# Local attention: the fourth spreading of key factors one step later, as the first dense product of step 14

## The reference

```python
qkv = shift_token(x) @ wqkv                    # 128 -> 3 x 512: 8 heads of 64
q, k, v = split(qkv)
q = l2norm(q) * qs
k = l2norm(k) * ksc
q, k = rotary_xpos(q, k)
o = local_attention(q, k, v)                   # window of 64, looks one window back, softmax
x = x + o @ wo
h = layernorm(shift_token(x)) ; h = h @ w1 + b1 ; a, g = split(h)
x = x + (a * gelu(g)) @ w2 + b2
```

## Time and profile before

| what | value |
|---|---|
| median of the runs | 4783.61 us (3 runs, 4780.45 to 4787.08) |
| the profiled execution, its own time | 4792.77 us |
| its span | 4791.0 us |
| mean granted clock of TensorE | 0.90 of full speed |
| first pass of the local attention | about 762 to 1272 us of the span |
| second pass | about 1804 to 2312 us |

### The profile page before, as it was taken

How to read it: one execution, slowest core, us unless ns; L and a number is a source line. 1 busy time by engine, 2 the same in 40 slices (tenths; PEclk the granted TensorE clock), 3 DMA queues, 4 the chain that set the end, 5 groups by cost and what they waited for, 6 DMA issues and landing times.

```text
span 4791.0 us, 62689 instructions
## 1 busy us (share of the span) xinstructions
PE 4206.6 (88%) x23278; PEld 2009.3 (42%) x23280; DVE 3025.6 (63%) x6690; ACT 2453.2 (51%) x4189; POOL 1123.7 (23%) x1579
## 2 busy tenths in 40 slices
PE   8888879999898889999886777999888999889999
PEld 5212335555522235555552224555553334333343
DVE  4888467667478867776345994666666653466622
ACT  3587634455348774554345553455444663236642
POOL 1100123333210013333112662111121004420034
PEclk9799987899879998998797998999997999969999
DMA  1100102111010011111000000000001000000000
GB/s 49 27 15 14 45 3 73 28 36 35 6 55 18 15 49 36 32 34 28 5 7 5 0 0 16 8 16 8 16 33 27 22 8 1 29 22 21 15 0 9
DMA packets 48017, 104.07 MB, mean 22 GB/s; under 512 B 15064, under 2 KB 15064, under 8 KB 46432
## 3 DMA queue, kind: packets, MB, share of 16 engines
q1 hardware_dynamic: 46560, 98.49, 7.5%
q10 hardware_dynamic: 1152, 1.57, 0.1%
HBM read 40.24 MB, written 1.05 MB: 9 GB/s over the span
## 4 chain that ended last, share of the span: by engine, by line
PE 62%; DVE 23%; ACT 8%; POOL 3%; issue 2%; DMA 1%; ACTq 1%; SPq 0%; POOLq 0%; DVEq 0%
PE PS L447 29%; PE PS L1123 8%; PE PS L1071 7%; DVE SM L1197 6%; PE PS L1103 3%; PE PS L2638 2%; DVE AR L2442 2%; ACT AR L454 2%; DVE AR L451 2%; PE PS L1741 1%; PE PS L1751 1%; PE PS L474 1%; PE PS L1076 1%; ACT AR L1171 1%; PE PS L1744 1%
## 5 line engine op out<-in xcount | busy, mean ns | idle before, releaser
L1197 DVE TENSOR_REDUCE SM<-PS 128x1 f32<-128x512 f32 (+3 forms) x1792 | 1028.3, 626 | 241.1 <-PE PS L1071 160.3
L447 PE MATMUL PS<-AR,WS 128*128 128x512 f32 (+1 forms) x2112 | 1058.1, 640 | 77.1 <-DVE AR L451 30.8
L1171 ACT ACTIVATE AR<-PS 128x1024 f32<-128x1024 f32 (+3 forms) x896 | 825.5, 933 | 342.5 <-PE PS L1106 171.6
L454 ACT ACTIVATE AR<-PS 128x512 f32<-128x512 f32 (+4 forms) x728 | 440.5, 614 | 523.4 <-PE PS L447 395.2
L1071 PE MATMUL PS<-AR 51*128 51x512 bf16 (+3 forms) x1792 | 527.6, 391 | 142.3 <-DVE SM L1197 98.9
L447 PEld LDWEIGHTS PS<-AR,WS 128*128 128x128 f32 (+1 forms) x2112 | 401.4, 202 | 539.0 <-issue 407.7
L1822 ACT ACTIVATE AR<-PS,SM 128x128 f32<-128x128 f32 x512 | 229.6, 452 | 475.3 <-DVE SM L1885 471.2
L1123 PE MATMUL PS<-AR 128*32 128x512 f32 (+3 forms) x3584 | 451.3, 577 | 1.3 <-ACT AR L1171 0.9
L1071 PEld LDWEIGHTS PS<-AR 51*128 51x128 bf16 x1792 | 130.0, 94 | 661.5 <-DVE SM L1197 476.2
L1103 PE MATMUL PS<-AR 51*128 51x512 bf16 (+3 forms) x1792 | 387.2, 367 | 11.8 <-ACT AR L1171 11.0
L1230 POOL CAST MBT<-SM 128x8 bf16<-128x8 f32 x128 | 28.0, 219 | 1262.7 <-DVE SM L1201 1065.8
(11 more groups left out here) (323 smaller groups left out, 7183.5 us busy)
## 6 DMA issues: line engine op xcount, KB each, us to landing
TP<-RAW SPq DMA_DIRECT2D x512, 64.0 KB, 2.0
AR<-AR SPq DMA_DIRECT2D x720, 32.0 KB
WS<-wall SPq DMA_DIRECT2D x4, 3654.5 KB, 11.2
WS<-wall SPq DMA_DIRECT2D x8, 902.5 KB, 4.5
WS<-wall SPq DMA_DIRECT2D x2, 3334.5 KB, 10.6
WS<-wall SPq DMA_DIRECT2D x1, 2384.0 KB, 9.2
WS<-wall SPq DMA_DIRECT2D x1, 1543.5 KB, 6.1
AR<-AR ACTq DMA_DIRECT2D x48, 32.0 KB
```

Source lines behind the costliest of these rows:

```text
L447: t = e.matmul(o, l, r, start=(n == 0), stop=(n == len(pairs) - 1))
L454: return e.activation(o, i, ACT.Copy, scale=1.0)
L1171: e.activation(pv[:, :, off:512], sv[:, :, off:512], ACT.Exp, scale=scale).then_inc(*F.at_exp.up((s, u, p2)))
L1197: e.tensor_reduce(mh[:, at, k0 // 512:k0 // 512 + 1], bank(ring(n + g), m), AX.X, ALU.max, negate=True).then_inc(*F.at_max.up((s, k, i, rr ...
```

## The change

For groups 1 to 7 `wide` 3 goes from `second` of step 13 to `first` of step 14. Group 0, which is prepared before the first unit, keeps its four in steps 13 and 14.

```diff
@@ -1622,10 +1622,15 @@
                 second = [("norm", g, j) for j, at in enumerate((2, 3, 4, 4, 6, 7, 10, 11)) if n == at] + second
                 if n == 11:
                     first += [("turn", g, 0)]
-                wide = 12 if g else 13
-                if n in (wide, wide + 1):
-                    first += [("wide", g, 2 * (n - wide))]
-                    second += [("wide", g, 2 * (n - wide) + 1)]
+                if n == 12 and g:
+                    first += [("wide", g, 0)]
+                    second += [("wide", g, 1)]
+                if n == 13:
+                    first += [("wide", g, 2 if g else 0)]
+                    second += [] if g else [("wide", g, 1)]
+                if n == 14:
+                    first += [("wide", g, 3 if g else 2)]
+                    second += [] if g else [("wide", g, 3)]
                 second += [("v", g, j) for j, at in enumerate((8, 11, 14, 15) if g else (8, 11, 12, 12)) if n == at]
```

## The result

The changed kernel takes 4754.6 us (median of 5 runs, 4750.2 to 4771.9) against 4783.9 us before (5 runs, 4780.5 to 4787.7): ratio 0.9949, 95% interval 0.9935 to 0.9963. A second set, taken beside the first experiments, gave 4761.8 us (12 runs, 4755.5 to 4775.8) against 4777.2 us (25 runs, 4764.2 to 4790.5): ratio 0.9970, interval 0.9958 to 0.9982. So the kernel is faster, by 29 us in one set and by 15 us in the other.

What follows compares the result with a forecast made beforehand. TensorE, 88% busy, was taken as the bound, waiting 27.3 us for VectorE's key products. Wait -21.1, border +1, clock -7 give -27.1 us; from the 4783.6 us median that makes 4756.5 us, range 4741 to 4773.

Steps and rivals of the forecast that it cites:

- The order and the removed wait: Steps 13 and 14: fourth spreading moves behind step 14's scores; TensorE's 27.3 us of key-product waits go or fall near 1 us.
- The second condition, the copy: Step 14's transposes must await VectorE's copy of step 13, so the shown group gains 1.8 us, not 1.95.
- The border: Product 3 in step 15 delays the next group's first scores, mostly hidden: 1 us for 14 borders, at most 10.
- The clock: Low clock from step 13 on ends 1.8 us sooner per group, 23 us in all; at 0.3 that gains 7 us.
- the 21.1 us: TensorE's gain from the removed wait over 14 groups, limited by the copy; bounds about 12 and 27.3 us.
- The low stretch halved: Rival: low-clock time from step 13 on halves, gaining 22 us instead of 7, total 4741.5 us; chance 0.15.
- That the clock would not move: Rival: the same light steps remain, transposes do not raise the clock, so no clock gain, 4763.5 us; chance 0.18.
- VectorE as the bound: Rival: border costs 10 us and step 15's copy delays step 0's transposes 7 us; 4779.5 us, no change; chance 0.11.
- The slower case: Rival: low clock spreads over whole groups, 5.9 us each; with seven of fourteen hit, 4805 us; chance 0.04.

Runs made afterwards that it cites:

- bank4: Kernel before, instruction order unchanged, with only the fourth spreading of groups 1 to 7 put in PSUM bank 4: 4758.2 us, ratio 0.9953.
- step14_double: Kernel before with product 3 computed twice in VectorE's step 14, once into a scratch tile: 4781.7 us, ratio 1.0008.
- again: The changed kernel, unaltered, measured once more beside the other experiments against the kernel before: 4761.8 us, ratio 0.9970.
- before_fill: Kernel before with five unused matmuls on TensorE ahead of the fourth spreading in groups 1 to 7: 4765.0 us, ratio 0.9962.

## Why the prediction was right, point by point

**The forecast** was 4756.5 us with a range of 4741 to 4773; the two sets gave 4754.6 and 4761.8. In differences, 27.1 us were forecast and 29 and 15 measured. Both times lie inside the range. That the first set met the forecast within 2 us is in part luck: two terms of the sum were wrong in opposite directions, as said below, and the same program gained half as much in the second set.

**The order and the removed wait.** As forecast: 27.3 us of waits for the key products became 9.8 us in all. I had expected "near 1 us"; 8.4 us remain for product 0 (11.1 in the second set), since the scores and values of step 14 ran at the higher clock and TensorE reached the moved spreading sooner than at the 2.21 us that I took from the earlier trace rows. In the shown group scores and values took 1.4 us (934.25 to about 935.65) and the spreading waited for product 0 to end.

**The second condition, the copy.** This step of the working decided, and as a bound it held. Forecast for the shown group: transposes of step 14 right behind the copy, 1.8 us gained. Measured: 0.14 us behind the copy's end, steps 13 and 14 in 8.04 us instead of 9.86, 1.8 us less. bank4 showed the same bound with another cure, 1.52 us of wait for the copy. Over all 14 groups steps 13 and 14 went from 131.2 to 106.2 and 107.4 us, 25.0 and 23.8 us less, where the sum said 21.1. But only a small part of that is idle time saved. In the shown group TensorE idled 1.95 us before and 0.93 + 0.64 = 1.57 us after; the scores and values between took 1.4 us instead of 2.21, at the higher clock. Of its steps 13 and 14 some 8.2 us had the low clock before and 2.6 us after. Over all groups the low clock in these two steps fell from 95 us to 46 and 40.

**The border.** The waits of the first scores are 1.4 us in 9 times, at most 0.2 each where up to 0.7 was forecast; the cost was put at 1. That they are hidden behind ScalarE's copy fits the shown group, where its wait shrank from 0.53 to 0.16 us; over both passes that wait (L1751, then L1756, for L454) went from 18.7 us in 26 times to 17.3 in 30. Counted from the weight loads, step 15 became longer (43.0 us in all groups before, 49.3 and 50.5 after) and step 0 shorter (52.7, then 41.8 and 46.6), but that is mostly where the count puts the border: before, the weight load of step 0's mask ran ahead of its matmul (956.25 and 956.68 in the shown group), and now it waits with it for product 3 (943.59 and 943.62). From mask matmul to mask matmul step 15 took 47.8 us before, 47.4 and 49.4 after, and step 0 45.7, then 41.0 and 45.4.

**The clock.** The term was too small, by the amount of low clock and not by its price. I took the low stretch to end 1.8 us sooner, 23 us of low clock in all, and argued that the clock falls before the wait, so that taking the wait away does not keep it high. In the traces it is the start that moved: before, in 11 of the 14 groups the low stretch began at most 2.3 us behind the start of step 13, or earlier; in the changed kernel that was so in 5 groups and in 2, and in the others it began 4.3 us or more behind it, in step 14. The passes had 168 and 206 us of it against 250, and against 207 in the profile of the kernel with product 3 twice, which has the same order. So the low clock saved is anything from 0 to 82 us, by the pair that one takes; in steps 13 to 0 alone it is 41 to 64 us. The price taken, 0.3 us per us, is near the 0.31 (13.4 us for 43, the kernel before against its double) to 0.44 us that pairs of like programs show; the 0.18 that stood at its lower end came from two groups of unlike work (477 and 499 matmuls).

What the change saves without the clock comes out alike in two estimates. At equal low clock over the passes (step14_double and again, 207 and 206 us, though spread otherwise: 126 and 85 us of it in steps 13 to 0) it is 1003.9 - 994.9 = 9.0 us; and the idle time in the rows of waits fell by 11.0 us, in the second set by 27.3 - 11.1 - 1.5 - (11.9 - 5.1) = 7.9 us. With the 0.34 us per us of before_fill, an estimate for the passes is 11.0 + 82 x 0.34 = 38.9 us (measured 39.0) and 7.9 + 44 x 0.34 = 22.9 us (measured 22.4). So about half or more of the 21.1 us that I booked as the wait's own length is the clock's: it was reckoned with step 14 at 1.2 GHz as it stood in the trace, and before_fill shows that this clock goes with the wait. The sum came out because what one term had too much the other had too little. (Its lower bound, given as about 12 us, is 21.1 - 10 = 11.1; the range goes by 11.)

**The rivals.** The low stretch halved (0.15) is nearly what happened to the clock (139 to 75 and 85 us in steps 13 to 0), but not to the time, since the 21.1 us beside it held the clock already and TensorE at the higher clock ran into waits for VectorE: 8.4 us for product 0 and 6.5 us more for the copy. That the clock would not move (0.18) is not borne out in the moved steps, where the low clock fell in both profiles; over the whole passes the second profile's 206 us are no less than the 207 of step14_double, so there it can't be excluded. The Trainium skill, "TensorE: Matmul & The Clock Gate", Part 4 (PE-mode transpose), has it that transposes do not count towards the full clock; what moved up was scores, a spreading and transposes, and the low clock of these steps fell all the same. No run isolates the transposes, so the rule itself is not tested. VectorE as the bound (0.11), by a border that costs its full 10 us, did not come; VectorE does bind step 14, through the copy. The slower case (0.04), low clock over whole groups, did not come; the one group that had it lost it (69.0 to 58.8 us), which may be luck of timing: in the kernel before that low clock had begun 25 us ahead of step 13, ahead of anything that the change moves in that group.

**What stays open.** How the 29 and the 15 us of the two sets divide into the change and the chance of the clock: the idle time saved is 8 to 11 us, the rest goes with the low clock, and the same program had 168 and 206 us of that. Open too is why the low clock, over work that is the same up to the wait, begins in step 13 in some groups and later in others. The medians of the kernel before in four sets were 4783.9, 4777.2, 4783.3 and 4778.1 us.

## What to carry to other kernels

Ask of a wait on TensorE also which clock the work behind it had: here waits of 2 us cost about as much through the clock behind them as through themselves, and filling them with idle matmuls brought 18 us where removing them brought 15 to 29. When a wait is taken away, look for the second condition on the same engine (here the copy behind the two products) and then for why that engine was late at all; the change alone brought 15 to 29 us, with both of these mended it was 54. And a gain worked out with durations at the low clock is counted again if the clock is a term of its own.

## What the runs showed of the hardware

- Five useless matmuls in each of 14 waits made the kernel 18 us faster, with a granted clock of 0.92 and 0.93 in the passes in place of 0.88 and 0.87.
- One program's two passes took 967.5 and 945.0 us in two profiles, another's 978.3 and 994.9; the granted clock (0.89 and 0.94, 0.94 and 0.94; 0.91 and 0.92, 0.90 and 0.89) went with it, while the rest of the spans differed by 6 and 1 us (4749.2 and 4720.5; 4752.8 and 4770.4).
- A VectorE operation of 0.16 to 0.18 us with two inputs in SBUF took 0.6 to 1.14 us when it met GpSimd's sum, and when it was moved away the next one of its kind met it. All 32 long ones of one line (of 93) began while a GpSimd instruction ran.
